# Flamingo block on one core: the scaled inputs of every second state made on TensorE by diagonal matrices of B

## What is computed

```python
x   = silu(causal_conv4(ctx @ in_proj.T) + conv_b)            # [4, 512 channels, 512 steps]
dt_low, B, C = split(x_proj @ x)                              # 16, 16 and 16 rows of 512 steps
dt  = softplus(dt_proj @ dt_low + dt_proj_b)                  # [4, 512, 512]
for n in range(16):                                           # each state n on its own
    h[n, t] = exp(dt * A[n])[t] * h[n, t-1] + (dt * x * B[n])[t]
y   = sum_n h[n] * C[n] + D * x
x1  = inp + tanh(g_xattn) * (y * silu(layernorm(inp)))
out = x1 + tanh(g_ffn) * (top2_experts(layernorm(x1)) + shared_expert(layernorm(x1)))
```

## Time and profile before

| | before |
|---|---|
| median of 3 runs | 1016.52 us (1015.74 to 1017.32) |
| the profiled execution | 1012.7 us |
| its span, first to last instruction | 1010.9 us |
| mean granted TensorE clock | 0.957 of 2.4 GHz |

### The profile page before, as it was taken

The page is one execution under the profiler, slowest core; times in us unless marked ns, Lnnn a source line. Parts: engine busy times, 40 slices in busy tenths (PEclk is TensorE's granted clock), DMA queues, the critical chain, the costliest instruction groups (busy, mean ns, idle before and its releaser), DMA issues.

```text
span 1010.9 us, 20635 instructions
## 1 busy us (share of the span) xinstructions
PE 891.2 (88%) x5397; PEld 752.7 (74%) x5397; DVE 738.8 (73%) x1112; ACT 593.1 (59%) x1006; POOL 571.0 (56%) x504
## 2 busy tenths in 40 slices
PE   6898789887988878877999999899999999974796
PEld 3465677566756767766999999899999898863795
DVE  5888989999999999999676676444554554555376
ACT  3669989797989999893332133334544444543121
POOL 5246996888968998987011057232534534531363
PEclk9799979999999999999999999999999999995699
DMA  8106111420115114113111157654657766664476
GB/s 278 44 21 229 33 42 43 154 89 31 53 38 205 42 48 135 44 49 120 42 42 42 53 174 297 213 191 168 232 182 237 238 184 237 227 199 132 139 246 225
DMA packets 65870, 136.39 MB, mean 135 GB/s; under 512 B 8833, under 2 KB 13441, under 8 KB 65666
## 3 DMA queue, kind: packets, MB, share of 16 engines
q1 hardware_dynamic: 54528, 104.68, 31.9%
q0 software_dynamic: 8960, 29.37, 8.1%
q10 hardware_dynamic: 2306, 1.33, 0.6%
HBM read 162.48 MB, written 42.07 MB: 202 GB/s over the span
## 4 chain that ended last, share of the span: by engine, by line
PE 33%; SPq 5%; POOL 5%; issue 5%; ACT 2%; DVE 2%; ACTq 1%; DMA 1%; POOLq 0%; DVEq 0%
PE psY L993 10%; PE psG L957 9%; PE psU L957 9%; POOL slot_in L641 3%; PE psT L950 2%; PE psHT L971 2%; POOL weights L666 1%; SPq L469 1%; SPq L525 1%; SPq L524 1%; ACT weights L1258 1%; SPq L526 1%; SPq L463 1%; SPq L509 1%; DMA xin<-xn_rows 1%
## 5 line engine op out<-in xcount | busy, mean ns | idle before, releaser
L597 POOL TENSOR_TENSOR prod<-hst,cbc 128x512 f32<-128x512 f32 x256 | 327.4, 1312 | 76.6 <-PE y_ps L804 39.5
L1507 DVE TENSOR_TENSOR_SCAN hst<-dA,dbu_ps 128x512 f32<-128x512 f32 x256 | 298.8, 1202 | 20.1 <-issue 10.1
L782 PE MATMUL dbu_ps<-ident,dbuT 128*128 128x128 f32 x1008 | 165.6, 288 | 45.9 <-DVE hst L1507 37.0
L782 PEld LDWEIGHTS dbu_ps<-ident,dbuT 128*128 128x128 f32 x1008 | 115.0, 145 | 107.8 <-DVE hst L1507 68.3
L1305 ACT CAST hh<-psHT 128x384 fp32r<-128x384 f32 x79 | 37.8, 478 | 252.8 <-PE psHT L971 252.8
L1179 ACT ACTIVATE dbuT<-duT,BT 128x512 f32<-128x512 f32 x252 | 160.7, 709 | 17.5 <-PE dbu_ps L782 15.6
L1169 ACT ACTIVATE dA<-dts,Aneg 128x512 f32<-128x512 f32 x256 | 166.4, 709 | 0.2
L804 PE MATMUL y_ps<-ident,prod 128*128 128x128 f32 x1024 | 159.1, 281 | 6.0 <-POOL prod L597 5.3
L957 PE MATMUL psU<-weights,xh 128*128 (+2 forms) x560 | 142.8, 337 | 0.0
L957 PE MATMUL psG<-weights,xh 128*128 (+1 forms) x560 | 137.7, 328 | 4.4 <-DVE xl L1756 3.8
L993 PE MATMUL psY<-weights,hh 128*128 (+3 forms) x420 | 134.1, 400 | 5.7 <-DVE hl L1750 3.3
(11 more groups left out here) (218 smaller groups left out, 1341.7 us busy)
## 6 DMA issues: line engine op xcount, KB each, us to landing
...
```

The source lines that it names most:

```text
L597: pool.tensor_tensor(prod[:, prod_slot(n, j), :], hst[:, slot_of(n, j), :], cbc[:, n % 2, :], ALU.mult).then_inc(prod_ready, 1)
L782: last = tr(dbu_ps[j % 2][:, t * P:(t + 1) * P], dbuT[:, n % 2, t, j * P:(j + 1) * P], ident[:])
L1507: V.tensor_tensor_scan(hst[:, slot_of(n, j), :], dA[:, slot_of(n, j), :], dbu_ps[j % 2][:], 0.0, ALU.mult, ALU.add).then_inc(scanned, 1)
```

## The change

For odd n the input term is made in another way. ScalarE scales the identity instead of duT: `diagB[:, t, :] = ident * B[n]`, four copies of 128x128 (one for each tile of 128 steps). TensorE multiplies: `dbu_ps = duT[:, t, block j].T @ diagB[:, t]`, a true matmul that turns and scales at once. Even n is as before. So dbuT needs one buffer, and diagB is the other half of the alternation. In batch 0 the diagonals of state 1 are made ahead of the copies of duT. The table PLAN is another one in every batch: among the differences, in batch 0 the table's entry conv (1, 2, 1) has two matmul items and four taps in place of eight and one; in the third batch du_copy and z_copy go to ScalarE; `terms` of the second batch is 0 and that of the last -1.

```diff
--- before.py
+++ after.py
@@ -98,7 +98,8 @@
         diag = s1("diag", [P, ND, P])
         Aneg = s1("Aneg", [P, ND, NS])
         BT = s1("BT", [P, 2, NL, XR])
-        dbuT = s1("dbuT", [P, 2, NL, D])
+        dbuT = s1("dbuT", [P, NL, D])
+        diagB = s1("diagB", [P, NL, P])
         dA = s1("dA", [P, RING, L])
 
         win_raw = dA[:, 0:2, :].rearrange("p a (k c) -> p (a k) c", c=DM)
@@ -332,29 +333,29 @@
 
 
         PLAN = (
-            dict(skip=7, silu=21, x_proj=(19, 20, 21, 22), xdbl=22, bt=33, bt_copy=33, dt=(23, 27, 37, 44),
-                 softplus=(25, 31, 45, 49), rounds=(24, 31, 41, 44), log=(23, 30, 39, 44),
-                 dt_sum=(26, 36, 42, 49), du=(26, 37, 44, 51), du_turn=(30, 43, 51, 55),
-                 du_copy=(30, 43, 51, 55), du_on_act=False,
-                 conv=[(1, 0, 0, (-1, -1, -1, -1, -1, -1, -1, -1), (-1,)), (2, 0, 1, (25, 26), (26, 27, 28, 29)), (2, 1, 1, (35, 36), (40, 40, 41, 42)), (1, 1, 0, (0, 1), (5, 5, 6, 7)), (1, 2, 1, (1, 2, 3, 4, 5, 6, 7, 8), (12,)), (1, 3, 0, (11, 12), (13, 13, 14, 15))],
-                 ctx=(14, 17), ctx_copy=(15, 17), z_turn=(46, 47, 53, 57), z_copy=(51, 54, 58, 62),
+            dict(skip=6, silu=17, x_proj=(16, 17, 18, 19), xdbl=20, bt=26, bt_copy=27, dt=(23, 30, 35, 44),
+                 softplus=(27, 35, 41, 50), rounds=(24, 31, 39, 48), log=(23, 31, 38, 48),
+                 dt_sum=(26, 34, 42, 52), du=(29, 34, 45, 53), du_turn=(31, 40, 49, 59),
+                 du_copy=(31, 40, 49, 59), du_on_act=False,
+                 conv=[(1, 0, 0, (-1, -1, -1, -1, -1, -1, -1, -1), (-1,)), (2, 0, 1, (19, 20), (23, 23, 24, 25)), (2, 1, 1, (32, 33), (37, 37, 38, 39)), (1, 1, 0, (2, 3), (4, 4, 5, 6)), (1, 2, 1, (4, 5), (4, 4, 5, 6)), (1, 3, 0, (8, 9), (9, 9, 10, 11))],
+                 ctx=(13, 16), ctx_copy=(14, 16), z_turn=(42, 44, 50, 57), z_copy=(44, 49, 59, 60),
                  z_on_act=True, terms=-1),
-            dict(skip=9, silu=17, x_proj=(16, 17, 18, 19), xdbl=19, bt=34, bt_copy=34, dt=(21, 29, 38, 42),
-                 softplus=(24, 35, 42, 45), rounds=(25, 35, 39, 49), log=(25, 34, 37, 46),
-                 dt_sum=(28, 37, 41, 54), du=(31, 39, 52, 57), du_turn=(32, 47, 52, 59),
-                 du_copy=(32, 47, 52, 59), du_on_act=False,
-                 conv=[(2, 2, 1, (7, 8), (7, 7, 8, 9)), (2, 3, 0, (6, 7), (7, 7, 8, 9)), (3, 0, 1, (26, 27), (28, 28, 29, 30)), (3, 1, 1, (36, 37), (37, 37, 38, 39))],
-                 ctx=(15, 22), ctx_copy=(15, 23), post=7, z_turn=(41, 50, 57, 58), z_copy=(45, 55, 60, 62),
-                 z_on_act=True, stats=(9, 13, 24, 63), terms=-1),
-            dict(skip=5, silu=17, x_proj=(15, 16, 17, 18), xdbl=19, bt=24, bt_copy=24, dt=(23, 29, 37, 47),
-                 softplus=(25, 32, 40, 53), rounds=(24, 32, 43, 50), log=(23, 31, 42, 47),
-                 dt_sum=(26, 35, 46, 52), du=(32, 37, 50, 55), du_turn=(37, 45, 56, 58),
-                 du_copy=(37, 45, 56, 58), du_on_act=False,
-                 conv=[(3, 2, 1, (8, 9), (9, 9, 10, 11)), (3, 3, 0, (4, 5), (5, 5, 6, 7))], post=3,
-                 z_turn=(27, 30, 46, 48), z_copy=(27, 35, 47, 53), z_on_act=False, stats=(18, 25, 37, 60),
+            dict(skip=7, silu=19, x_proj=(16, 17, 18, 19), xdbl=19, bt=30, bt_copy=30, dt=(21, 32, 37, 45),
+                 softplus=(25, 36, 40, 53), rounds=(22, 32, 38, 51), log=(21, 30, 37, 49),
+                 dt_sum=(28, 35, 42, 55), du=(30, 38, 53, 58), du_turn=(33, 45, 55, 60),
+                 du_copy=(33, 45, 55, 60), du_on_act=False,
+                 conv=[(2, 2, 1, (8, 9), (9, 9, 10, 11)), (2, 3, 0, (6, 7), (6, 6, 7, 8)), (3, 0, 1, (24, 25), (25, 25, 26, 27)), (3, 1, 1, (35, 36), (35, 35, 36, 37))],
+                 ctx=(15, 18), ctx_copy=(15, 18), post=5, z_turn=(44, 50, 53, 56), z_copy=(48, 54, 55, 63),
+                 z_on_act=True, stats=(11, 18, 21, 41), terms=0),
+            dict(skip=5, silu=17, x_proj=(15, 16, 17, 18), xdbl=18, bt=37, bt_copy=37, dt=(19, 25, 33, 46),
+                 softplus=(22, 29, 34, 52), rounds=(19, 29, 34, 50), log=(18, 28, 37, 48),
+                 dt_sum=(24, 32, 44, 57), du=(32, 34, 53, 58), du_turn=(34, 44, 54, 60),
+                 du_copy=(39, 49, 61, 62), du_on_act=True,
+                 conv=[(3, 2, 1, (7, 8), (9, 9, 10, 11)), (3, 3, 0, (4, 5), (4, 4, 5, 6))], post=3,
+                 z_turn=(21, 25, 41, 48), z_copy=(23, 30, 47, 59), z_on_act=True, stats=(30, 36, 39, 43),
                  terms=-1),
-            dict(skip=5, silu=11, conv=[], post=3, z_turn=(9, 20, 31, 40), z_copy=(15, 29, 35, 45), z_on_act=True,
-                 terms=0),
+            dict(skip=6, silu=15, conv=[], post=4, z_turn=(15, 17, 31, 44), z_copy=(17, 27, 43, 46), z_on_act=True,
+                 terms=-1),
         )
 
         USE0, USE1 = {}, {}
@@ -778,8 +779,14 @@
                 if j == 0:
                     pe.wait_ge(dbut_ready, b * NS + n)
                 pe.wait_ge(scanned, i - 1 + RING)
+                if b == 0 and n == 1 and j == 0:
+                    pe.wait_ge(first_dut, ND)
                 for t in range(NL):
-                    last = tr(dbu_ps[j % 2][:, t * P:(t + 1) * P], dbuT[:, n % 2, t, j * P:(j + 1) * P], ident[:])
+                    if n % 2 == 0:
+                        last = tr(dbu_ps[j % 2][:, t * P:(t + 1) * P], dbuT[:, t, j * P:(j + 1) * P], ident[:])
+                    else:
+                        last = mm(dbu_ps[j % 2][:, t * P:(t + 1) * P], duT[:, b % 2, t, j * P:(j + 1) * P],
+                                  diagB[:, t, :], start=True, stop=True)
                 last.then_inc(dbu_ready, 1)
 
             def add_skip(b):
@@ -876,7 +883,7 @@
                 if j >= 2:
                     pe.wait_ge(scanned, j - 1 + RING)
                 for t in range(NL):
-                    last = tr(dbu_ps[j % 2][:, t * P:(t + 1) * P], dbuT[:, 0, t, j * P:(j + 1) * P], ident[:])
+                    last = tr(dbu_ps[j % 2][:, t * P:(t + 1) * P], dbuT[:, t, j * P:(j + 1) * P], ident[:])
                 last.then_inc(dbu_ready, 1)
 
             def first_block(*parts):
@@ -1175,14 +1182,20 @@
                     act.wait_ge(misc_read[1], USE1["du", b, ND - 1] + 2)
 
                 act.wait_ge(dbu_ready, (b * NS + n + 1) * ND)
+                if b == 0 and n == 1:
+                    act.wait_ge(first_bt, 1)
                 for t in range(NL):
-                    last = nc.scalar.activation(dbuT[:, n % 2, t, :], duT[:, b % 2, t, :], ACT.Copy,
-                                                scale=BT[:, b % 2, t, RK + n:RK + n + 1])
+                    if n % 2 == 0:
+                        last = nc.scalar.activation(dbuT[:, t, :], duT[:, b % 2, t, :], ACT.Copy,
+                                                    scale=BT[:, b % 2, t, RK + n:RK + n + 1])
+                    else:
+                        last = nc.scalar.activation(diagB[:, t, :], ident[:], ACT.Copy,
+                                                    scale=BT[:, b % 2, t, RK + n:RK + n + 1])
                 last.then_inc(dbut_ready, 1)
 
             def step(b, n):
                 terms = PLAN[b]["terms"]
-                if terms < 0:
+                if terms < 0 and (b, n) != (0, 1):
                     input_terms(b, n)
                 for j in range(ND):
                     decay(b, n, j)
@@ -1242,6 +1255,7 @@
                 first_parts(j)
             decay(0, 0, 0)
             first_parts(ND - 1)
+            input_terms(0, 1)
             for j in range(ND):
                 first_copy(j)
                 if j + 1 < ND:
@@ -1538,9 +1552,9 @@
                     post(b - 1)
                 if b == 0 and i < 6:
                     z_stat(NL + 6 + i)
+                if b == 0 and i == 6:
+                    z_var(0, NT, 0)
                 if b == 0 and i == 10:
-                    z_var(0, NT, 0)
-                if b == 0 and i == 16:
                     z_scale()
                 if 0 < b < NB - 1:
                     for t in range(NL):
@@ -1634,7 +1648,7 @@
 
                 dve.wait_ge(first_full, 13 + j)
                 dve.wait_ge(first_bt, 1)
-                V.tensor_tensor(dbuT[:, 0, :, j * P:(j + 1) * P],
+                V.tensor_tensor(dbuT[:, :, j * P:(j + 1) * P],
                                 first_du[j][:].rearrange("p (t d) -> p t d", t=NL),
                                 BT[:, 0, :, RK:RK + 1].broadcast_to([P, NL, P]), ALU.mult).then_inc(first_term, 1)
 
```

## The result

The changed kernel takes 1027.12 us (median of 4 runs, 1026.07 to 1030.01), the kernel before, run beside it, 1016.92 us. The ratio is 1.0106, 95% interval 1.0078 to 1.0133: slower by 1.1%, some 11 us. The forecast was 1024.5 us, in a range of 1009 to 1032.

The account below looks back on a forecast made before the run. VectorE was taken to bound the scan part (94% busy). State sums +15.7, reach -5, bare items +2, ScalarE -3, start -2.7 and batch boundary +1 gave +8 us: median 1024.5 us, range 1009 to 1032.

Parts of the forecast that it names:

- booked at -3: Scan part: ScalarE, relieved of 41 us by smaller odd-state copies, makes VectorE wait less; -3 us, bounds 0 and -8.
- The start: Start of the scan part: convolution steps leave TensorE's work before scan 4, diagB is ready early; -2.7 us, bounds 0 and -2.9.
- The table: New PLAN in the scan part: VectorE's own sum falls 2.9 us, with eight third-batch copies moved to ScalarE (-5.0).
- the queue at item 62: Batch boundary: the third batch's last du copy stands in ScalarE's queue ahead of later work, shortening VectorE's reach; +1 us.
- The records: Odd items: true matmuls issue eight records, not four; states where TensorE's work is larger go from 9.4 to 28.2 us over.
- state sums: Scan part, per state: the larger of VectorE's and TensorE's work is taken; 397 us for the old table, 413 for the new.
- corrected by -5 and +2: Scan part: -5 us for TensorE one item ahead after VectorE's extra steps, +2 for bare items in some 12 odd states.
- credit of 5 us for TensorE's reach: A VectorE step ending a state leaves TensorE one item ahead, paying part of the next state's excess; -5 us.
- VectorE's busy time: Scan part: VectorE's own sum was to fall by 2.9 us, from 388 to 385.
- (1) VectorE hides the matmuls: Rival, odd states: VectorE's extra steps cover TensorE's excess, leaving -8.6 us, 1008 us; chance 0.22.
- (2) The clock: Rival, scan part: a busier TensorE never falls to half clock, -7 us on top of +8, 1017.5 us; chance 0.13.
- (3) Half clock on odd states: Rival, scan part: odd items at 1.2 GHz need 2.7 us of TensorE, up to +10 us, 1031 us; chance 0.10.

Follow-up runs that it names:

- e3: The kernel before with each transpose of an odd state's input term issued twice, ScalarE not relieved; ratio 1.0182 to the kernel before.
- e5: The changed kernel with transposes of unscaled duT in odd states, 4 records an item, not 8 (scale B left out); ratio 0.9972 to the kernel before.
- e4: The kernel before with ScalarE's odd-state copies cut to 128x128, one block transposed for all four (result incomplete); ratio 1.0013 to the kernel before.
- e2: The kernel before with the new table and earlier layer-norm steps, transposes and full copies in every state; ratio 1.0028 to the kernel before.
- e10: The kernel before with only the third batch's four z copies moved from VectorE to ScalarE; ratio 1.0050 to the kernel before.
- e1: The kernel before, its table kept, with diagonals and true matmuls in odd states, and early diagonals of state 1; ratio 1.0203 to the kernel before.
- e8: The kernel before with diagonals in 19 states, the second batch's new table entry, third batch's z copies on ScalarE; ratio 1.0086 to the kernel before.
- e9: As e8, but no diagonals in the second batch (14 states stay) and the third batch's z copies on VectorE; ratio 1.0058 to the kernel before.

## Why the prediction was right, and where its terms were wrong

**The bound and the mechanism.** It was forecast that odd items need 1.34 us of TensorE against 1.12 of a bare scan, that VectorE's idle would rise from 26 to some 37 us, and that TensorE ends it. Measured 1.33 us a bare odd scan, 38.2 us idle. By the profile's names TensorE's groups end 10.9 us of the scans' waits and ended 7.0; 2.4 us more have no named releaser, and some 3 us more lie in gaps too short for that view (the scans' idle time rose from 20.1 to 31.4 us in all). The records came as forecast: 1024 for 512 matmuls, 0.89 us a group, 0.111 us each. The 60 us more for TensorE are 55 in the busy time of its weight loads (279.1 to 334.2), 37 in that of its matmuls. e3 and e5 show that it is these records: doubling transposes costs 19 to 22 us, halving the change's records gives back 12 to 15.

**ScalarE.** The small copy: 0.32 us forecast; the group has 389 ns as the mean of one, and four in a row take 1.28 us, as was booked for a state. By the formula of the Trainium skill ("ScalarE: Activation LUTs", What ACT_TABLE_LOAD costs), without its overlap, one of 128 elements is an estimated 386 ns; the row agrees. With its 93 ns of overlap each further one adds an estimated 0.29 us, and a row of four takes 1.27 us; the measured 1.28 agrees. The copies of all states took 160.7 us before and 119.9 after (79.2 and 40.7), the forecast 41 us less. ScalarE's busy time fell by 34.6 us, forecast 36. Its worth was booked at -3, bounds 0 and -8: it measured nothing on the table of before (e4, 1.0013) and -6.0 on the new one (e2 to e5). Both lie inside the bounds, and the booked value was right for neither.

**The start.** Scan 4 was forecast near 53.6 us, from 56.3; it came at 54.3. So 2.0 of the 2.7 us.

**The table, a wrong term.** The sum gave the table -2.9 us (VectorE's work), -2.7 (start) and +1 (du copy), -4.6 in all. Measured +2.9 by the whole times and +7.9 by the scan part (e2): wrong in sign by either. The step that failed is the one that counted copies moved to ScalarE as VectorE's gain of 5 us, beside a ScalarE that I held to be idle enough. It is in-order waiting that made ScalarE late: e10 shows it for four copies on the table of before (+5.1 us), the 3.80 us stall of e2 for the new one. The prediction named the queue at item 62 for 1 us; it should have asked the same of each of the eight moved copies.

**The records, near in size on this table alone.** The state sums gave them 18.8 us, corrected by -5 and +2 to about 16. Measured on the new table 11.8 by the scan parts and 14 to 15 by the whole times; on the old one 22 to 23, and 19 to 20. For both tables the state sums give nearly the same, some 20 us, so they can't tell why the old table pays 5 to 11 us more. The credit of 5 us for TensorE's reach fits the new table and not the old, where e1 came 8 us over what this sum expected. One part may be the clock: on the new table the records cut the time at half clock from 44.4 to 20.5 us, on the old one from 37.5 to 23.9. At the 0.2 us lost for each us at half clock (VectorE idle 6.0 of 34.2 us), this is about 5 against 3 us, and so 2 us of the difference. That is an estimate, not measured; the rest stays open.

**VectorE's busy time** was to fall by 2.9 us and rose by 1.7. The scans did most of it: 298.8 to 302.9 us for the same 256 (the twelve `du` steps added 1.5). Back to back they overlap in the record (seven in 7.87 us, are 1.12 each; alone one is 1.20 to 1.22), and a scan that waits loses that 0.07 to 0.1 us. It is part of the price of every wait that the sum left out.

**The total.** By the scan parts the measured terms are table +7.9, relief -6.0, records +11.8, together +13.7 us. By the whole times they are +2.9, -5.8 and +13.6, together +10.7, as the ratio has it. Those of the forecast were -4.6, -3 and +16, with rounding +8. So the table was 7.5 to 12.5 us too low, the relief 3 and the records 2 to 4 too high: the forecast came near partly by luck, because its errors stood against each other. The end of the scans came at 482.6 us, not 477. The medians differ by 10.2 us and the profiled executions by 14 (1012.7 and 1026.76): that of before lay 4 us under its median, that of the changed kernel at its own.

**The rivals.** (1) VectorE hides the matmuls: no, by the 1.33 us period; where I put them by the state sums it was true in two batches (e8, e9). (2) The clock: its direction was right, since half-clock time fell from 34.1 to 20.5 us, but the 13.6 us are worth an estimated 3 us by the same 0.2, not 7, and they are inside what the records measured. (3) Half clock on odd states: five pieces remain in the changed kernel, and single stalls show it (eight records in 1.76 us there, in 1.83 us in e9), but with 20.5 us at half clock in all, less than before, the total isn't theirs.
